# Local attention layers of a one-core kernel: queries, keys and values of a pair of heads in one projection, value chunks copied by DMA, the first maxima in the pair's own position

## The reference, cut to what matters

```python
for i in range(DEPTH):                                   # DEPTH = 6, called twice
    x = attn_layer(shift_tokens(x), Wqkv[i], q_scale[i], k_scale[i], Wo[i]) + x
    x = ffn_layer(shift_tokens(x), ln_g[i], ln_b[i], W1[i], b1[i], W2[i], b2[i]) + x

def attn_layer(x, Wqkv, qs, ksc, Wo):
    q, k, v = split(x @ Wqkv)                            # 16 heads of 64
    q, k = l2norm(q) * qs, l2norm(k) * ksc
    q = q * cos * scale + rotate_half(q) * sin * scale   # k with 1 / scale
    out = local_attention(q, k, v)                       # softmax over a window: own 32 tokens and the 32 before
    return out.transpose(0, 2, 1, 3).reshape(b, n, INNER) @ Wo
```

## Time and profile before

| | |
|---|---|
| median of 3 runs | 5900.51 us (5897.06 to 5904.95) |
| span of the profiled execution | 5900.4 us |
| busy: TensorE, its weight loads, VectorE, ScalarE, GpSimd | 5495.2, 3949.3, 4294.8, 4093.6, 2762.7 us |
| first local stage | from about 1033 to 3247 us of the span |
| second local stage | from about 3690 us to the end |

### The profile page before, as it was taken

One profiled execution on the slowest core, in us unless ns is written; L12 is line 12 of the kernel. 1 busy time (PEld: TensorE's weight loads), 2 busy tenths in 40 slices (PEclk: granted clock), 3 DMA queues, 4 the chain that ended last, 5 costly groups with the idle time before them and its releaser, 6 DMA issues. The chain is left out here.

```text
span 5900.4 us, 159891 instructions
## 1 busy us (share of the span) xinstructions
PE 5495.2 (93%) x60258; PEld 3949.3 (67%) x60258; DVE 4294.8 (73%) x6692; ACT 4093.6 (69%) x7768; POOL 2762.7 (47%) x2483
## 2 busy tenths in 40 slices
PE   8998986899999999999998899899999999999998
PEld 3334443678777777777776333677777778777776
DVE  7876654777777777777775886777777777777775
ACT  5774654677777777777775577677777777777775
POOL 1101100566655665556663110566556666556663
PEclk8997998899999999999999899999999999999999
DMA  0000000100000000000000000100000000000000
GB/s 13 2 2 6 2 3 8 36 17 16 19 14 19 17 16 20 15 18 16 16 21 10 4 2 2 36 17 16 20 13 19 17 16 21 16 17 16 17 20 18
DMA packets 128857, 87.46 MB, mean 15 GB/s; under 512 B 33332, under 2 KB 121936, under 8 KB 128056
## 3 DMA queue, kind: packets, MB, share of 16 engines
q1 hardware_dynamic: 128056, 76.74, 4.6%
HBM read 68.96 MB, written 1.05 MB: 12 GB/s over the span
## 5 line engine op out<-in xcount | busy, mean ns | idle before, releaser
L1733 POOL TENSOR_TENSOR cross<-raw,tab_b 128x512 f32<-128x512 f32 x768 | 998.1, 1324 | 304.6 <-ACT raw L1600 301.8
L737 DVE TENSOR_REDUCE arena<-PS 128x1 f32<-128x512 f32 (+3 forms) x1408 | 828.4, 646 | 216.4 <-PE PS L550 130.5
L1739 POOL CAST kT_b<-kT 128x512 bf16<-128x512 f32 x384 | 311.9, 812 | 1318.2 <-ACT kT L1656 1318.2
L688 ACT ACTIVATE arena<-PS 128x1024 f32<-128x1024 f32 (+1 forms) x704 | 668.4, 968 | 203.1 <-PE PS L573 126.3
L1853 DVE TENSOR_TENSOR oT<-PS,rec_den 128x288 f32<-128x288 f32 (+1 forms) x768 | 326.2, 425 | 635.2 <-ACT rec_den L1634 635.2
L1824 DVE TENSOR_TENSOR rot<-PS,tab_a 128x512 f32<-128x512 f32 x768 | 521.9, 686 | 227.9 <-PE PS L1451 133.8
L1406 PE MATMUL PS<-qT,kT 64*128 64x96 f32 x8448 | 660.6, 287 | 0.0
L1626 ACT ACTIVATE PT<-PS 128x576 f32<-128x576 f32 (+1 forms) x768 | 468.7, 610 | 257.9 <-PE PS L1406 245.3
L1600 ACT COPY raw<-PS 128x512 f32<-128x512 f32 x768 | 447.1, 589 | 285.5 <-PE PS L1451 244.8
L1840 DVE TENSOR_TENSOR rot<-rot,cross 128x1024 f32<-128x1024 f32 x384 | 613.4, 1597 | 17.8 <-POOL cross L1733 17.4
L1847 DVE TENSOR_TENSOR rot<-rot,inv_norm 128x1024 f32<-128x1024 f32 x384 | 578.6, 1507 | 10.6
(11 more groups left out here) (260 smaller groups left out, 13084.0 us busy)
## 6 DMA issues: line engine op xcount, KB each, us to landing
w_qk<-in_w_pairs SPq DMA_DIRECT2D x196, 128.0 KB, 2.1
w_v<-in_w_pairs SPq DMA_DIRECT2D x100, 128.0 KB, 2.2
w_o<-in_w_out_pairs SPq DMA_DIRECT2D x192, 64.0 KB, 1.9
xs<-staged SPq DMA_DIRECT2D x24, 224.0 KB, 2.6
w<-in_L_ffn_W SPq DMA_DIRECT2D x12, 341.0 KB
q_parts<-max_rows SPq DMA_DIRECT2D x192, 2.0 KB
V<-in_c_E SPq DMA_DIRECT2D x2, 896.0 KB, 8.3
w<-in_L_ffn_W SPq DMA_DIRECT2D x24, 64.0 KB
```

Of the source, the lines that this page charges most:

```text
L688: nc.scalar.activation(PT[u % 6].rearrange("p (a n) -> p a n", a=2)[:, :, first_q:512], PS[:, 2 * (u % 2):2 * (u % 2) + 2, first_q:512], A ...
L737: nc.vector.tensor_reduce(maxima[:, 2 * m + h, qt, kh:kh + 1], bank[:, 0:keys_of(qt, kh)], AX.X, ALU.max).then_inc(bank_free, 1)
L1733: nc.gpsimd.tensor_tensor(dst[:, :, :, o:o + 32], src[:, :, :, other:other + 32], tab[:, :, o:o + 32].unsqueeze(2).broadcast_to([128, 8, 2 ...
```

## The change

1. **One projection.** `w_qkv`, 384 columns, takes the place of `w_qk` and `w_v`. `projections` replaces `query_keys`: each tile fills a bank of its own with 384 of its 512 columns, so a pair has eight fills (Q0 to Q7) instead of four. The 132 value matmuls of a batch, ScalarE's copies of V and the split of `w_v` are gone. The split of `w_qkv` has 384 columns.
2. **Two banks are released at once.** ScalarE copies two banks at a time, 2 x 384 columns, to `raw`, which now has 384 columns a tile, and `by_cosine` reads two banks and releases both with one semaphore count (`filled_pair`, `leader`, `release_of`).
3. **V by DMA.** `gather_values` copies the values out of `raw` into the chunk layout `V[p % 2]` with seven transfers inside SBUF, 1344 rows of 512 bytes. SyncE issues them in each position, behind w_o, the staged rows and the scales, and ahead of the weights. The copy of the next pair's first tiles to `raw` waits for them, as does the pair's first `values`.
4. **First group's maxima in the pair's own position.** `maximum(…, 0)` and `maxima(…, 0)` stand at the end of the position in which K and q of the pair are made. The second group stays behind the next position's first four tiles.
5. The staging of constants moves from V to other tiles.

```diff
-            names = (["Q0", "Q1"] if a else []) + (["x0", "x1", "x2", "x3"] if bb else []) + (["Q2", "Q3"] if a else [])
+            names = (["Q0", "Q1", "Q2", "Q3"] if a else []) + (["x2", "x3"] if bb else []) + (["Q4", "Q5", "Q6", "Q7"] if a else [])
             for slot in (0, 5, 1, 2, 3, 4):
                 names += late_names(l, b, p, slot)
-            return names
+            return names + (["x0", "x1"] if a else [])
...
+            def filled_pair(eng, l, b, p, i):
+
+                need(eng, full, fill(l, b, p, f"Q{2 * i + 1}") + 1)
+                bank = bank_of(l, b, p, f"Q{2 * i}")
+                return PS[:, bank:bank + 2, 0:384], free[bank]
...
+                def gather_values(p):
+
+                    for r, key, rows, tile, at, first, n in ((0, 0, 32, -1, 96, 1, 2), (0, 32, 96, 0, 0, 0, 3), (1, 0, 64, 0, 64, 0, 3), (1, 64, 64, 1, 0, 0, 3),
+                                                             (2, 0, 96, 1, 32, 0, 3), (2, 96, 32, 2, 0, 0, 2), (3, 0, 128, 2, 0, 0, 2)):
+                        c, t = 4 * first + r, 3 * first + tile
+                        sp.dma_start(V[p % 2][key:key + rows, c:c + 4 * n - 3:4, :], raw[at:at + rows, t:t + 3 * n - 2:3, 256:384]).then_inc(values_in, 16)
...
-                        need_apart(sp, wqk_split, it * 2 + 4)
+                        need_apart(sp, pv_full, it * 4 - 4)
+                        need_apart(sp, raw_in, it * 4 + 4)
+                        gather_values(p)
+                        need_apart(sp, wqkv_split, it * 2 + 4)
...
-                def query_keys(l, b, p, i):
+                def projections(l, b, p, i):
...
-                    bank = bank_for(l, b, p, f"Q{i}")
-                    for j in range(2):
-                        t = 2 * i + j
+                    for t in range(2 * i, 2 * i + 2):
+                        bank = bank_for(l, b, p, f"Q{t}")
                         for n, (m, w) in enumerate(PRODUCTS):
-                            last = nc.tensor.matmul(bank[:, 256 * j:256 * j + 256], x_parts[b][m][:, PAD + 128 * t:PAD + 128 * t + 128], wqk_parts[w][:, :],
+                            last = nc.tensor.matmul(bank[:, 0:384], x_parts[b][m][:, PAD + 128 * t:PAD + 128 * t + 128], wqkv_parts[w][:, :],
                                                     start=n == 0, stop=n == 2)
-                    last.then_inc(full, 1)
+                        last.then_inc(full, 1)
...
                     if bb:
-                        maximum(l, b, p, 0)
                         maximum(l, b, p, 1)
...
+                    if a:
...
+                        maximum(l, b, p, 0)
...
                 def raw_copy(l, b, p, i):
                     need(act, cross_done, item(l, b, p) * 4 + (2 * (i // 2) - 2))
-                    bank, _ = filled(act, l, b, p, f"Q{i}")
-                    nc.scalar.copy(raw[:, 2 * i:2 * i + 2, :].rearrange("p t n -> p (t n)"), bank).then_inc(raw_in, 1)
+                    if i == 0:
+                        need(act, values_in, item(l, b, p) * GATHERS)
+                    banks, _ = filled_pair(act, l, b, p, i)
+                    nc.scalar.copy(raw[:, 2 * i:2 * i + 2, :], banks).then_inc(raw_in, 1)
```

229 lines of the change are left out of this document (115 added, 114 removed).

## The result

| | |
|---|---|
| before, median of 4 runs | 5901.0 us (5897.1 to 5905.0) |
| after, median of 4 runs | 6333.5 us (6332.7 to 6337.1) |
| ratio | 1.073, 95% interval 1.072 to 1.075 |
| forecast | 6120 us, range 5860 to 6230 |

A forecast was written before the change was run, and what follows sets the result against it. TensorE's queue was taken as the bound before, the chain through each position after the change. 5900.5 + 149 (chain) + 72 (gather) = about 6120 us, slower by 3.7%; range 5860 to 6230.

The forecast's parts named there:

- sum two: Local layers, eight positions a batch: time added through the dependency chain, +6.2 us a batch, +149 us in all.
- the chain: Each position's sequence: projections, copy to `raw`, `cross`, `rot` add and normalise, transposes, quotients, third values; +149 us.
- sum one: TensorE's own work in the local layers: 8.8 us added, 17.8 removed a batch; net -216 us if TensorE stayed the bound.
- the removed work of the values: 132 value matmuls a batch gone from TensorE, with ScalarE's value copies; about -132 us in the forecast, as a remainder.
- the projections with their banks: Two rows of twelve 384-column matmuls a position, 1.98 and 2.18 us for 1.43 and 1.62; +213 us.
- the gather's place: V transfers late in SyncE's queue in position 1 of batch 1, delaying position 2's first copy 6.0 us; +72 us.
- K0: TensorE's transposes of the first half of `rot`; in even positions they would wait 1 to 2.5 us for the normalise.
- the 0.74 us of moved maxima: First group's maxima leave the time ahead of K0 and cost 0.74 us at the position's end.
- The clock: Rival 5: TensorE's stop in position 2 of batch 1 brings 1.2 GHz, 48 us more, 6168 us; chance 0.05.
- the forecast's case: Rival 3, the forecast's own mechanism in local layers and gather, sizes within the ends: 5980 to 6200 us; chance 0.56.
- TensorE-bound and faster: Rival 1: K0 of even positions takes no wait, value matmuls' time stays won; 5756 us, half 5850; chance 0.18.
- rival 4: V transfers in front of the projections' copies, 0.86 us issue each, +70 us: 6190, up to 6250; chance 0.07.

The follow-up runs named there:

- the ladder: Table of differences between run medians, one part of the change at a time, leading from the kernel before (5901 us) to the changed kernel (6333 us).
- before_no_v: The kernel before without any work for the values (V matmuls, their copies, the split and loads of `w_v`): 5863.7 us, 0.993.
- before_no_v_warm: The kernel before without any work for the values, plus nine unread matmuls in positions 0 and 2: 5815.3 us, 0.985.
- gather_first: The changed kernel with SyncE's seven gather transfers issued at the head of each position: 6227.5 us, 1.055.
- rows_early: gather_first with the row-maxima matmuls ahead of the projection's last two tiles and ScalarE's copy to R ahead of its last `raw` copy: 6147.0 us, 1.042.
- old_maxima: gather_first with the first group's maxima moved back behind the next position's first four tiles: 6161.6 us, 1.044.

## Why the prediction was wrong, step by step

**The step that failed is sum two, +149 us for the chain, where the runs have +326 (6227 - 5901).** The miss is not in sum one, which the forecast didn't use. By the ladder two terms of sum two were mis-sized: what the removed work of the values gives back, booked at about -132 us and worth -37, and the projections with their banks, booked at +213 us and worth 156 + 136. With the gather's place, 106 for 72, that is 95 + 79 + 34 = 208 of the 213 us that were missing. The sums of the ladder are measured; that the booked terms fall to its steps in this way is worked out, not tested.

**The removed work.** The chain gave it little ahead of K0, rightly, but full price elsewhere (0.45 us behind K0 in position 6; 0.4 and 0.8 in odd ones; ScalarE's 1.2 in position 4). before_no_v shows why it was worth less: where the V matmuls stood, TensorE then waits for PT (130.8 us) and for R (89.3 us), and its clock stands at 1.2 GHz for 282 us instead of 58. With the clock held up (before_no_v_warm) the same work is worth 85 us. Sum one had it larger still, with 0.135 us a matmul. TensorE's busy time in before_no_v_warm, at clock 0.99, is 162.5 us a batch, of which 18 unread matmuls are 3.6: 158.9 against 173.4, so 132 matmuls were 14.5 us, 0.110 each. TensorE's busy time was to fall by some 200 us; it rose by 16, in part because more of it ran at the lower clock.

**The projections.** A 384-column matmul was priced at 0.165 and costs 0.175, the straight line of the earlier trace rows that I had set aside for a lower value. The 24 of a position were to take 1.11 us more and took 1.5, of which 0.6 to 0.7 came from a bank for each tile, which was in no term. In the middle layers of gather_first `raw` is complete 7.48 us after a position's start in all positions but 4 and, in batch 0, 0 (forecast 7.1), the first half is ready at 13.1 in positions 2 and 6 (12.7), and Y0 starts at 7.3 to 7.4 (6.85; the prediction's own terms give 5.1 + 0.95 + 0.69 = 6.74). So this one term made the whole chain 0.4 us late. In positions 5 and 6 that is most of the 0.6 us by which they missed.

**K0 and the order of the lock.** K0 waits for `rot` in position 6, 0.85 us where 1 to 2.5 was forecast; with R (1.04) and PT (0.17) TensorE waits 2.06 us ahead of K0, where the prediction had 2.3, all at K0. From the complete `raw` to the first half it took 5.6 us in after, as the prediction's steps had it (12.7 - 7.1). But that holds only while GpSimd's last product starts ahead of VectorE's add. By rows_early (copy 0.5 us later, K0 0.5 earlier) and old_maxima (copy 0.95 us later, K0 the same) a later copy turns the order round and K0 does not follow it. The prediction had seen that the two take turns, and then took the turn's order as fixed. So it counted the 0.74 us of moved maxima as a gain ahead of K0 and a cost at the end, and called the move nothing in sum; in position 6 only the cost was real, and old_maxima puts the move at 66 us in all.

**The wait for R was left out** in even positions, where it was 1.04 us; in odd ones it was put at 0.5 and was 0.4 in positions 1, 3 and 5. With 130 us in all it is the largest wait of the changed kernel. Before, V matmuls stood in exactly that place. In position 6 it lay in time that TensorE had to wait for K0 anyway. rows_early takes it away, and most of Y0's wait with it, and gave 80 us for both. The same holds for the wait for PT, 105 us, which the prediction doesn't name.

**The positions.** Forecast +6.2 a batch. Of gather_first, without the queue's effect, it was +14.3 (193.3 + 194.6 - 178.3 - 181.0, halved). In most it was about twice the forecast or more (position 1 +1.8 for +0.9, 2 +3.4 and +2.8 for +1.5, 3 +1.2 for +0.4, 5 and 6 +1.2 for +0.6, 7 of batch 0 +2.1 for +1.5); none had the wrong sign. Position 0 of batch 0, +3.4 for +0.5, and position 7 of batch 1, +3.6 for +1.5, have the jump of the loop in or behind them, and positions 0 and 2 the low clock, neither of which was in the sum.

**The gather.** Mechanism and place were right. That the copy came 6.0 us late, as forecast, is in part luck: the transfers were issued at 0.63 us each (median of 1344) where 0.45 was taken, and the first copy went 7.1 us after the first issue instead of 5.5; but the queue was free 0.6 us earlier than forecast and position 1 was 1.0 us longer, so less of it showed. In gather_first position 2 of batch 1 is 7.7 us shorter and that of batch 0 1.2, together twelve times 8.9 = 107 us, for 72 forecast. In batch 0 the prediction's own numbers gave 28.9 - 4.3 - 22.9 = 1.7 us late, not "at most 1"; it was 2.1. The rest of batch 1's 7.7 stands beside a clock of 0.83 in after and 0.93 in gather_first.

**The clock** was a rival of its own at +48 and a chance of 0.05. It came together with the forecast's case: 343 us at 1.2 GHz against 58. At the two measured prices, 0.17 and 0.32, the 285 us more are some 50 to 90 us (an estimate), spread over several steps of the ladder, the gather's 106 among them. By the Trainium skill's rule ("TensorE: Matmul & The Clock Gate", Part 1), cited there, the array falls to half its clock after idling, so that the stop had to be paid; the rows at 4939.44, 0.32 us apart, agree.

**The rivals.** TensorE-bound and faster (0.18) needed K0 without a wait; it waits. Its share was too high for a kernel in which the trace showed VectorE's half only 0.5 us ahead of TensorE. The upper end of the range, 6230, came from one rival alone. The prices of rivals 4 and 5 can be paid together: forecast, rival 4's large gather and the clock would have given 6120 + 70 + 48 = 6238, and with the chain's upper end 6305, still short of 6333.

## What to carry to other kernels

Work taken off a full engine is worth its time only if no wait stands behind it in the same place. Before crediting removed instructions, look at what each block separates, and ask when its successor's operands are ready; a trace in which the engine never idles does not show those waits, and leaving the work out in one run prices them (here 40 us for the 427 of sum one). A transfer that others wait for goes to the head of its queue, ahead of loads that are wanted a stage later.

## What the runs showed of the hardware

- Low clock was cheaper than its length: each us at 1.2 GHz that unread matmuls took away gave back 0.17 us in one kernel and 0.32 in the other. Waits of about a microsecond can bring it without a long stop: in position 2 of before_no_v TensorE waits 2 to 4 us in all, never more than 1.5 at a time, and the clock falls in 15 of the 22 such positions behind the first. In the other seven the same waits pass at 2.4 GHz. Before, with 1.0 us of waits in that position, it hardly fell.
- SyncE issued the SBUF-to-SBUF transfers of V in 0.63 us each (median; 0.60 at least), longer than its weight load, 0.34 us (0.33 at least). They landed 2.3 us after their issue.
- Behind the jump back of the loop TensorE stood idle 3.6 to 4.5 us in after, where the 22 bfloat16 matmuls of the maxima came last, and 1.9 to 2.5 us before and 1.9 to 2.3 in old_maxima, where eight transposes did. The last instructions don't settle it: before_no_v has transposes there too, and 3.1 to 3.3 us at three of its eight jumps. Why is open.
- Which of two engines goes first can hang on 0.1 us, and a later input can then make a result come no later or even earlier. In after the add began about 0.1 us behind GpSimd's product and took 2.27 us; in old_maxima it began ahead and took 1.33.
